# Eight turned sums spread among the gate and up products of the single chunk, in the first step of each half of a feed forward

## The reference

```python
gate = jnp.einsum('bsh,ih->bsi', x, gate_w) * gate_scale
up = jnp.einsum('bsh,ih->bsi', x, up_w) * up_scale
inter = jax.nn.silu(gate) * up
out = jnp.einsum('bsi,hi->bsh', inter, down_w) * down_scale
```

## Time and profile before

| | |
|---|---|
| median of 3 runs | 1645.33 us (1645.15 to 1645.78) |
| the profiled execution | 1645.85 us |
| its span in the trace | 1644.0 us |
| PE busy | 1615.2 us, 98% of the span |
| DVE, ACT, POOL busy | 71%, 57%, 51% of the span |
| granted clock of PE, page part 2 | 9 (tenths, 9 is 90% or more) in all 40 slices |
| feed forward | from 1292 us of the span to its end |

### The profile page before, as it was taken

How to read it: one execution, slowest core, us unless ns; L and a number is a source line. 1 busy time by engine, 2 the same in 40 slices (tenths; PEclk the granted TensorE clock), 3 DMA queues, 4 the chain that set the end, 5 groups by cost and what they waited for, 6 DMA issues and landing times.

```text
span 1644.0 us, 26456 instructions
## 1 busy us (share of the span) xinstructions
PE 1615.2 (98%) x8298; PEld 1368.8 (83%) x8298; DVE 1163.2 (71%) x2988; ACT 936.2 (57%) x2480; POOL 830.8 (51%) x1243
## 2 busy tenths in 40 slices
PE   7999999999999999999999999999999999999999
PEld 5778887888888888888888888888888788878887
DVE  7963365776776776777677767767767688787676
ACT  5865455665665765765666566657657443434432
POOL 6852004544634634644545445446446397709752
PEclk9999999999999999999999999999999999999999
DMA  5002753111111111134111111111111121102211
GB/s 187 24 18 83 282 197 123 39 65 39 52 65 39 52 64 39 44 100 183 47 52 39 65 40 52 65 39 52 65 40 26 41 70 64 39 32 91 64 65 52
DMA packets 62490, 114.99 MB, mean 70 GB/s; under 512 B 5584, under 2 KB 25040, under 8 KB 58256
## 3 DMA queue, kind: packets, MB, share of 16 engines
q1 hardware_dynamic: 62352, 113.30, 20.8%
HBM read 84.97 MB, written 28.31 MB: 69 GB/s over the span
## 4 chain that ended last, share of the span: by engine, by line
PE 90%; DVE 5%; issue 2%; ACT 1%; POOL 1%; DMA 1%; DVEq 0%; SPq 0%; POOLq 0%; ACTq 0%
PE ps_q L1912 21%; PE ps_q L1852 19%; PE f_ps_r L2393 11%; PE ps_o L1894 8%; PE f_ps_y L2412 7%; PE ps_s L1870 5%; PE ps_s L1882 5%; PE ps_s L1868 3%; PE kv_banks L1280 3%; PE kv_banks L1290 3%; PE kv_banks L1299 3%; PE f_ps_r L2377 1%; DVE bn_ln L97 1%; DVE h_lo L74 1%; DVE x L744 0%
## 5 line engine op out<-in xcount | busy, mean ns | idle before, releaser
L1912 PE MATMUL ps_q<-kv_w_hi,o_hi 128*128 128x512 f32 x512 | 202.2, 395 | 0.0
L1912 PE MATMUL ps_q<-kv_w_lo,o_hi 128*128 128x512 f32 x512 | 199.7, 390 | 0.0
L1912 PE MATMUL ps_q<-kv_w_hi,o_lo 128*128 128x512 f32 x512 | 199.6, 390 | 0.0
L74 POOL TENSOR_TENSOR kv_w_lo<-w_raw,kv_w_hi 128x512 fp32r<-128x512 f32 x128 | 163.2, 1294 | 56.3 <-ACT kv_w_hi L69 56.2
L1852 PE MATMUL ps_q<-h_hi,kv_w_hi 128*128 128x512 f32 x448 | 180.1, 402 | 0.1
L1852 PE MATMUL ps_q<-h_lo,kv_w_hi 128*128 128x512 f32 x448 | 175.1, 391 | 0.0
L1852 PE MATMUL ps_q<-h_hi,kv_w_lo 128*128 128x512 f32 x448 | 175.0, 391 | 0.0
L1681 DVE TENSOR_TENSOR x<-ps_q,x 128x512 f32<-128x512 f32 x128 | 88.1, 688 | 96.4 <-PE ps_q L1912 96.4
L69 ACT ACTIVATE kv_w_hi<-w_raw 128x512 fp32r<-128x512 f32 (+1 forms) x240 | 126.7, 567 | 45.5 <-POOL w_raw L300 42.0
L1495 ACT ACTIVATE prob<-prob,neg_max 128x128 f32<-128x128 f32 x256 | 100.4, 392 | 89.3 <-DVE neg_max L1651 89.3
L1440 POOL TENSOR_SCALAR prob<-prob,inv_sum 128x128 f32<-128x128 f32 x256 | 95.4, 373 | 109.5 <-DVE inv_sum L1656 109.4
(11 more groups left out here) (236 smaller groups left out, 4844.3 us busy)
## 6 DMA issues: line engine op xcount, KB each, us to landing
w_raw<-in_wq_g SPq DMA_DIRECT2D x16, 1024.0 KB, 4.8
w_raw<-in_wo_g SPq DMA_DIRECT2D x16, 1024.0 KB, 4.7
k_raw<-k_scratch SPq DMA_DIRECT2D x32, 256.0 KB, 3.4
v_raw<-v_scratch SPq DMA_DIRECT2D x32, 256.0 KB, 3.8
f_gate_raw<-in_gate_c SPq DMA_DIRECT2D x10, 512.0 KB, 4.9
f_up_raw<-in_up_c SPq DMA_DIRECT2D x10, 512.0 KB, 3.6
f_down_raw<-in_down_c SPq DMA_DIRECT2D x10, 512.0 KB, 4.1
x<-in_x SPq DMA_DIRECT2D x16, 256.0 KB, 2.8
```

The costliest lines, as they stand in the source:

```text
L74: return dve.tensor_tensor(parts[LO], src, parts[HI].bitcast(F32), ALU.subtract)
L1912: done = pe.matmul(ps_q[:, half, :], o[b][i][:, half, h, :], wo[j][:, h, :], start=(h == 0 and m == 0), stop=(h == GROUP - 1 and m == 2))
```

## The change

The eight T fills no longer stand in one row between G1 and U0. One list gives the order of the twelve fills of the step, and PE, ACT and DVE each walk it: G0, T0, T1, T2, G1, T3, T4, U0, T5, T6, U1, T7. The banks follow from the new order, and so do the fills that `freed` waits for. In the second half the high part of the single up weight comes on ACT behind silu G0, where it came behind silu G1. What ACT issues behind the loop (`given("G", k + 1)` and on) stays behind the loop. POOL's and SP's programs are the same.

```diff
+        MINGLED = (("G", 0), ("T", 0), ("T", 1), ("T", 2), ("G", 1), ("T", 3), ("T", 4), ("U", 0), ("T", 5), ("T", 6), ("U", 1), ("T", 7))
+
         fills = []
         for k in range(STEPS):
             half, b = at(k)
-            for kind in "GU":
-                if b == 0 and kind == "U":
-                    fills += [("T", half, pos) for pos in range(8)]
-                if b == 0:
-                    fills += [(kind, k, n) for n in range(2)]
-                else:
-                    fills += [(kind, k, name) for name in CHAIN]
+            if b == 0:
+                fills += [(kind, half if kind == "T" else k, n) for kind, n in MINGLED]
+            else:
+                fills += [(kind, k, name) for kind in "GU" for name in CHAIN]
...
             def first_step(k):
 
-                for n in range(2):
-                    await_fill(act, "G", k, n)
-                    silu(k, n, bank("G", k, n))
-                if k:
-                    given("U", k)
-                for pos in range(8):
-                    turned(k // WIDE, 1, pos)
+                for kind, n in MINGLED:
+                    if kind == "T":
+                        turned(k // WIDE, 1, n)
+                    elif kind == "G":
+                        await_fill(act, "G", k, n)
+                        silu(k, n, bank("G", k, n))
+                        if k and n == 0:
+                            given("U", k)
                 given("G", k + 1)
                 gate.made_hi(act, k + 1)
                 down_part(k)
...
             def first_step(k):
 
-                for pos in range(8):
-                    turned(k // WIDE, 1, pos)
-                for n in range(2):
-                    await_fill(dve, "U", k, n)
-                    multiply(k, n, bank("U", k, n))
+                for kind, n in MINGLED:
+                    if kind == "T":
+                        turned(k // WIDE, 1, n)
+                    elif kind == "U":
+                        await_fill(dve, "U", k, n)
+                        multiply(k, n, bank("U", k, n))
...
                 if k % WIDE == 0:
-                    alone("G", k)
-                    for pos in range(8):
-                        turn(k // WIDE, 1, pos)
-                    alone("U", k)
+                    for kind, n in MINGLED:
+                        if kind == "T":
+                            turn(k // WIDE, 1, n)
+                        else:
+                            alone(kind, k, n)
```

More of the change, by code:

```diff
@@ L2365, in freed, with alone @@
                     pe.wait_ge(summed[kind], sums(k, {"P6": "U2", "P2": "C11", "P7": "U3", "P4": "C21", "P5": "U4", "P3": "C12"}[name]))
-            def alone(kind, k):
+            def alone(kind, k, n):
                 w = weights[kind]
                 pe.wait_ge(w.lo_done, w.count(k))
[L2371 to L2379, removed]
+                freed(kind, k, n)
+                pe.wait_ge(feed.h_lo, feed.flips(k // WIDE, 0, 7))
+                for c in range(KC):
+                    right = feed.operand((("B11", "B12"), ("B21", "B22"))[c // 2][n])
+                    for m, (a, b) in enumerate(PASSES):
+                        last = pe.matmul(bank(kind, k, n), w.single[a][:, c * P:(c + 1) * P], right[b][:, c % 2, :],
+                                         start=(c == 0 and m == 0), stop=(c == KC - 1 and m == 2))
+                last.then_inc(r_done, 1)
             def products(kind, k):
```

## The result

The changed kernel takes 1659.38 us (median of four runs, 1657.71 to 1659.53) against 1645.55 us; the ratio is 1.0076, with a 95% interval of 1.0063 to 1.0088. It is slower by 12.5 us (10.4 to 14.5). The profiled execution has a span of 1657.7 us, 13.7 more than before.

What follows compares the result with a forecast made beforehand. PE bounds the kernel, with P6's start set by the gate weights' preparation. Delays of 5.48 and 3.97 us sum to +9.45 us, so 1645.33 + 9.45 = 1654.8 us; range 1653.5 to 1659.2.

Steps and rivals of the forecast that it cites:

- the wait: Delay of P6's start behind later gate weights: 5.48 us in the first half, 3.97 in the second, +9.45 in sum.
- The forecast's own case: Both halves late, clock unchanged: 1654.8 us, 1653.8 to 1656.0 with the scatter of the runs; chance 0.72.
- rival A: PE's clock falls in idle times around P1, slowing matmuls from P6 by 2.1 us each half: 1659.0 us; chance 0.20.
- P6 is bound by the preparation of the gate weights in both halves, before anything is changed: Ahead of P6 on PE: POOL's S2 low part ends the gap, about 0.27 us by issue starts in the first half.
- The new wait of G1 for silu G0: On PE, first half only: G1 takes G0's bank and waits for ACT's silu, a new wait of 0.96 us.
- From there no wait is left by my working: On PE, first half, from G1 to T7: every fill's needed part is ready before the fill is due.
- T7 and `given`: ACT's gate weights start behind T7's high part: at 1308.46 instead of 1302.98, and at 1482.91 instead of 1478.94.
- The gate chain from `given` to P6: ACT and POOL preparing gate weights: 6.62 us in the first half, 6.89 in the second, not shortened by starting later.
- POOL's odd wait of 0.43 us: Second half, ahead of making S2 on POOL: kept in the sum, with 0.3 us of it taken into the range.
- Behind P6 I let the rest shift as it is: After P6's start: later work moves along unchanged, and nothing gives the delay back.
- the clock's term: PE's pace after idle times around P1: no cost in the main sum; 2.1 us each half only if the clock fell.
- Rival B: The gate chain does not decide: P6 starts 0.47 and 2.25 us earlier, 1642.6 us, no slower; chance 0.03.

Runs made afterwards that it cites:

- e8_row_early: Kernel before, with given("G", k + 1) on ACT behind the high part of T4 in place of T7; ratio 0.9992 (0.9983 to 1.0001), -1.3 us.
- e4_busy: Changed kernel, with unread matmuls on PE ahead of the waits of P1 (14) and P6 (9); ratio 1.0059 (1.0044 to 1.0074), +9.7 us against before.
- e6_busy_second: Changed kernel, with 9 unread matmuls on PE ahead of P6's wait only; ratio 1.0079 (1.0062 to 1.0095), +13.0 us against before.
- e10_after: The changed kernel run again as it is; ratio to the kernel before 1.0068 (1.0054 to 1.0081), +11.2 us.
- e3_row_late: Kernel before, with ACT also waiting until U1 is multiplied before given("G", k + 1); ratio 1.0063 (1.0048 to 1.0078), +10.4 us.
- e1_early: Changed kernel, with given("G", k + 1) behind silu G1 and gate.made_hi behind T6's high part; ratio to before 0.9990 (0.9981 to 0.9999), -1.6 us.
- e9_best: Changed kernel with early gate weights, early one-column silu, T7 one product earlier and gate.made_hi behind T7; 1643.27 us beside 1646.66 before, ratio 0.9981.
- e7_t7_before_u1: Changed kernel with only the order altered, T7 one product earlier, ahead of U1; ratio to before 1.0034 (1.0022 to 1.0046), +5.6 us.
- e5_busy_first: Changed kernel, with 14 unread matmuls on PE ahead of P1's wait only; ratio 1.0071 (1.0056 to 1.0086), +11.7 us against before.
- e2_early_table: Changed kernel with early gate weights on ACT, plus a one-column silu at the feed forward's start; ratio to before 0.9984 (0.9976 to 0.9993), -2.6 us.

## Why the prediction was right, and where it fell short

The forecast was slower, by 9.45 us for the wait; the range's upper end, 1659.2, lies 0.2 below the median, and inside what the ratio gives (1645.3 x 1.0076 = 1657.8, 1655.7 to 1659.8). The direction and the wait came out as worked out. The forecast's own case, 1653.8 to 1656.0 us, did not: what the first runs measured, 12.5 us with 10.4 as its lower bound, is more than the wait, and the range reaches it only because it was drawn over rival A.

- "P6 is bound by the preparation of the gate weights in both halves, before anything is changed": shown by e8_row_early, in which the gaps ahead of P6 vanish when only those weights start earlier.
- The new wait of G1 for silu G0: put at 0.96 by starts, it is 1.01 by starts (1297.82 less the end of T2's turn, 1296.81; the profile's bracket has 0.85), and only in the first half. "From there no wait is left by my working": so it is in both halves; no T, U or G between G1 and T7 waits.
- T7 and `given`: from G0 to `given` 16.12 us expected (1308.46 - 1292.34), 16.25 measured; in the second half 15.07 and 15.16. Of the first half's 0.13, 0.06 is G1's later start; the rest, and the second half's 0.09, arises at the changes of operation and at the first matmul behind the wait. I took the changes as nothing within a bound of 0.6 for both halves.
- The gate chain from `given` to P6: 6.62 and 6.89 us expected, 6.53 and 6.81 measured. The two small errors cancel: 5.48 and 3.97 us of delay expected, 5.52 and 3.98 measured. POOL's odd wait of 0.43 us ahead of S2 in the second half came again at 0.43, so keeping it in the sum was right.
- "Behind P6 I let the rest shift as it is": true but for the clock. e4_busy, with the clock kept up, is late by 9.7 us as a whole and by 9.6 at P6.
- Rival A was given 0.20 and was the case, in both halves of the profiled execution. The failed step is the clock's term, which the main sum put at nothing: it measured 3.5 us in the first trace of the changed kernel and 4.4 in the second. It was left out on the argument that an idle time of 2.31 us elsewhere had left the pace alone. That row shows one outcome of something that comes out either way: in e6_busy_second the same idle time of 3.5 us ahead of P1 left the clock up in the first half and let it fall in the second. Its price was put at 2.1 us each half; it was 1.59 and 1.90, and in e10_after 2.58 and 1.78.
- In rival A's mechanism "P1 would take 2.6 us and still end before P6's weights": this is what e10_after (first half) and e3_row_late show. In the first trace of the changed kernel it came otherwise: in the second half only the end of P1 was slow, and in the first half P1 was not slow at all; there the clock fell 1.45 us after P6 had begun, in the midst of unbroken work.
- Rival B's gain is real once its condition is met: e1_early meets it. It put P6 0.47 and 2.25 us earlier than before; 0.03 and 1.86 came. It forgot that P6 also waits for the low part of T7, the last fill ahead of P1, which is 0.28 us of what is missing in each half.

The Trainium skill's rule on banks (page Perfetto Trace Analysis, section Matmuls) holds here as far as e9_best goes: with every low part beside a product no fill waits. The Trainium skill's rule on idle gaps (page TensorE: Matmul & The Clock Gate, section Why this matters for your kernels) agrees with the granted clock of 0.72 and 0.55 in the stretches around P6, and by it 1659.0 would have been the forecast. The first half of e6_busy_second does not agree with it: an idle time of 3.5 us left the granted clock at 1.00 there, and the measurement decides.

## What to carry to other kernels

Before an instruction is moved on one engine, list what stands behind its consumer on the next engine: here moving the last transposes behind two products moved eight preparations on ACT that have nothing to do with them, and of these were the ones that PE already waited for. The remedy is to start the longest chain of preparation as soon as its room is free; with that alone the change that cost 12.5 us gains 1.6 (0.2 to 3.1), and with the table and T7 moved as well 3.1 (1.6 to 4.6). A forecast that creates idle times like these on PE should carry the fall of the clock in its main sum: in the profiled executions here it came in nine of the twelve halves that had them, and cost from nothing to 2.8 us a half.

## What was not expected of the hardware

- The fall of the granted clock does not follow from the length of the idle time alone. The table has every half of a profiled execution with an idle time of PE around P1 (us, from start to start, less the matmul or transposes between), where its clock fell, and what that cost; "filled" is an idle time filled with the matmuls that nobody reads. What decides between a fall and none stays open.

| half | idle ahead of P1 | idle ahead of P6 | the clock fell | cost |
|---|---|---|---|---|
| changed, first | 3.5 | 2.2 | 1.45 us behind P6's start | 1.6 |
| changed, second | 3.5 | 2.3 | 1.0 us behind P1's start | 1.9 |
| e10_after, first | 3.5 | 1.0 | ahead of P1 | 2.6 |
| e10_after, second | 3.5 | 2.0 | 0.8 us behind P1's start | 1.8 |
| e3_row_late, first | 3.0 | 1.0 | ahead of P1 | 2.8 |
| e3_row_late, second | 3.0 | 1.3 | ahead of P1 | 0 (back at P6) |
| e7_t7_before_u1, first | 0.9 | 2.2 | some 0.9 us behind P6's start | 1.6 |
| e7_t7_before_u1, second | 0.9 | 2.5 | not | 0 |
| e5_busy_first, first | filled | 2.3 | not | 0 |
| e5_busy_first, second | filled | 2.6 | 0.3 us behind P6's start | 1.6 |
| e6_busy_second, first | 3.5 | filled | not | 0 |
| e6_busy_second, second | 3.5 | filled | ahead of P1 | 2.4 (P6 late) |

- The clock can fall after PE has been at work again: in the changed kernel's first half at 1317.0, 1.45 us behind the start of P6, for eight matmuls, up to 1320.4, with P1 and the first six matmuls of P6 at the full pace.
- The ACT table load of 1.28 us is not done while ACT waits: ACT is idle for 7.61 us ahead of it, and it begins only when G0 is done. A silu of one column ahead of it takes it off the path, 1.1 us in e2_early_table.
